# Linear attention in a decoder: the last third of a group's TensorE order is rewritten

## The reference, cut to what matters

```
q, k = split(x @ Wq.T), split(x @ Wk.T)             # 4 heads of 32
v    = split(x @ Wv.T)                              # 4 heads of 64
g    = log_sigmoid(x @ Wgk1.T @ Wgk2.T + bgk2) / 32 # decay of every token and channel
A[t, j] = sum_d q[t,d] * k[j,d] * exp(b[t,d] - b[j,d]),  j <= t,  b = cumsum(g)
o = A @ v
o = o * rsqrt(mean(o*o) + eps) * rms_w
x = layernorm(x + (o * silu(x @ Wg.T)) @ Wout.T)
```

## Time and profile before

| | us |
|---|---|
| median of 3 executions | 1483.53 |
| lowest and highest of them | 1474.55, 1489.40 |
| the profiled execution | 1490.95 |
| its span (first to last instruction) | 1489.10 |

### The profile page before, as it was taken

How to read it: one execution, slowest core, us unless ns; L and a number is a source line. 1 busy time by engine, 2 the same in 40 slices (tenths; PEclk the granted TensorE clock), 3 DMA queues, 4 the chain that set the end, 5 groups by cost and what they waited for, 6 DMA issues and landing times.

```text
span 1489.1 us, 63792 instructions
## 1 busy us (share of the span) xinstructions
PE 1276.1 (86%) x26566; PEld 845.5 (57%) x26566; DVE 1211.1 (81%) x2613; ACT 1048.7 (70%) x2244; POOL 801.3 (54%) x1590
## 2 busy tenths in 40 slices
PE   5899898998867777776666699999999999999896
PEld 2566556666544444443333367676766666666685
DVE  2567777676668988887999789999999999999765
ACT  2567676776657888776777667777777777777555
POOL 3366666676657877776888633344433333333133
PEclk8899999999978999888999999999999999999889
DMA  7000000000000000000000000000000000000012
GB/s 201 20 3 3 3 4 2 4 3 4 10 9 24 18 23 19 17 18 2 1 2 2 1 3 3 3 3 3 3 3 17 18 17 24 18 18 10 2 44 72
DMA packets 28671, 24.28 MB, mean 16 GB/s; under 512 B 3676, under 2 KB 23906, under 8 KB 28386
## 3 DMA queue, kind: packets, MB, share of 16 engines
q1 hardware_dynamic: 28386, 20.21, 4.9%
HBM read 15.94 MB, written 4.19 MB: 14 GB/s over the span
## 4 chain that ended last, share of the span: by engine, by line
PE 43%; POOL 23%; issue 18%; DVE 9%; ACT 6%; SPq 0%; POOLq 0%; DMA 0%; DVEq 0%; ACTq 0%
PE keys_T L591 8%; PE keys_O L572 5%; PE keys_O L578 4%; PE keys_E L486 3%; POOL gla_low L1157 3%; PE keys_S L331 3%; POOL cross_pairs L838 3%; POOL cross_spread L805 2%; DVE ffn_hh L2031 2%; PE keys_E L529 2%; POOL gla_gate L1183 2%; ACT keys_pT L658 2%; POOL gla_yg L1190 2%; PE keys_O L598 2%; POOL gla_sq L1177 2%
## 5 line engine op out<-in xcount | busy, mean ns | idle before, releaser
L340 POOL TENSOR_SCALAR keys_spread<-keys_kT,keys_heads 128x512 f32<-128x512 f32 x128 | 86.9, 696 | 230.1 <-ACT keys_kT L622 230.1
L658 ACT ACTIVATE keys_pT<-keys_T 128x512 f32<-128x512 f32 x256 | 152.3, 595 | 76.3 <-PE keys_T L591 73.0
L350 DVE TENSOR_REDUCE keys_mx<-keys_S 128x16 f32<-128x1024 f32 x128 | 156.1, 1219 | 16.4 <-PE keys_S L331 14.6
L591 PE MATMUL keys_T<-ident_sb,keys_pexp 128*128 128x128 f32 x1024 | 165.0, 284 | 3.2 <-ACT keys_pT L658 2.3
L353 DVE TENSOR_TENSOR keys_pe_in<-keys_S,keys_mx 128x1024 f32<-128x1024 f32 x128 | 156.7, 1224 | 4.4
L591 PEld LDWEIGHTS keys_T<-ident_sb,keys_pexp 128*128 128x128 f32 x1024 | 112.6, 141 | 72.5 <-ACT keys_pT L658 38.3
L674 ACT ACTIVATE keys_pexp<-keys_pe_in 128x1024 f32<-128x1024 f32 x128 | 134.7, 1053 | 0.0
L711 DVE RECIPROCAL keys_rinv<-keys_O 128x128 f32<-128x128 f32 x128 | 120.3, 940 | 0.0
L1656 DVE COPY_PREDICATED gla_at<-gla_node,gla_GP 128x256 f32<-128x256 int32 x128 | 65.6, 513 | 61.0 <-ACT gla_at L1502 57.7
L1157 POOL TENSOR_TENSOR gla_low<-gla_ex,gla_kT 128x128 f32<-128x128 f32 x160 | 72.7, 483 | 71.3 <-ACT gla_ex L1493 71.3
L572 PEld LDWEIGHTS keys_O<-keys_pT,keys_vz 128*32 128x32 f32 x4096 | 63.0, 109 | 64.2 <-ACT keys_pT L658 63.8
(11 more groups left out here) (290 smaller groups left out, 3775.2 us busy)
## 6 DMA issues: line engine op xcount, KB each, us to landing
context<-in_ctx_T SPq DMA_DIRECT2D x32, 256.0 KB, 2.7
xs<-in_x SPq DMA_DIRECT2D x8, 512.0 KB, 7.4
out_x<-xs SPq DMA_DIRECT2D x16, 256.0 KB, 2.3
keys_mask_q<-keys_mask_b SPq DMA_DIRECT2D x64, 1.0 KB
keys_bias_right_f<-in_alibi_right SPq DMA_DIRECT2D x1, 512.0 KB, 3.8
ffn_w<-in_L_ffn_w_gate_T SPq DMA_DIRECT2D x1, 256.0 KB, 4.6
ffn_w<-in_L_ffn_w_up_T SPq DMA_DIRECT2D x1, 256.0 KB, 4.7
ffn_w<-in_L_ffn_w_down_T SPq DMA_DIRECT2D x1, 256.0 KB, 5.4
```

Source lines behind the costliest of these rows:

```text
L340: nc.gpsimd.tensor_scalar(spread[:, :, :, j, :].rearrange("q t s k -> q (t s) k"), flat.rearrange("q (a k) -> q a k", k=SEQ), heads[:, j:j ...
L350: nc.vector.tensor_reduce(m, quads(S), X, ALU.max).then_inc(c["mx"], 1)
L591: last = nc.tensor.transpose(T[:, j * P:(j + 1) * P], pexp[:, t % 2, (4 * half + j) * P:(4 * half + j + 1) * P], sh.ident[:, :])
L658: nc.scalar.activation(pT[:, t % 2, 4 * half:4 * half + 4, :].rearrange("q n k -> q (n k)"), T[:, :], ACT.Copy).then_inc(c["pT"], 1)
```

## The change

TensorE: the long product of tile 2 moves from bank EB to bank OB and behind the transposes of the group before; the long product of tile 3 moves behind the decay sums of tile 0; the output product of the group before moves from between the decay sums of tiles 0 and 1 to between two pieces of the next gram, which is issued in levels (0, 1), (2, 3), (4, 5) instead of (0, 1, 2), (3, 4, 5). ScalarE's copies move to match.

```diff
--- before.py
+++ after.py
@@ -1387,8 +1387,6 @@
                     gram(g, p, 1, (2, 3), closes=True)
                 ahead(2)
                 if n:
-                    c.await_nth(pe, "kT", g + 1, 1, 1)
-                    values_and_gates(g + 1, 1 - p, 2, EB)
                     c.await_nth(pe, "vg", g + 1, 2, G)
                 if l:
                     if not n:
@@ -1398,16 +1396,13 @@
                 if n:
                     if m:
                         await_pair(pe, "o", g, 0, 1, 1)
-                    else:
-                        c.await_nth(pe, "vg", g + 1, 1, G)
-                    values_and_gates(g + 1, 1 - p, 3, OB)
-                    c.await_nth(pe, "vg", g + 1, 3, G)
+                    values_and_gates(g + 1, 1 - p, 2, OB)
+                    c.await_nth(pe, "kT", g + 1, 1, 1)
                     if l:
                         await_pair(pe, "yT", g - 1, 1, 1, 1)
                     decay_sums(g + 1, 1 - p, 0)
-                if l:
-                    output(g - 1, 0)
-                if n:
+                    c.await_nth(pe, "vg", g + 1, 3, G)
+                    values_and_gates(g + 1, 1 - p, 3, OB)
                     c.await_nth(pe, "ex", g + 1, 1, G)
                     decay_sums(g + 1, 1 - p, 1)
                 if m:
@@ -1417,10 +1412,14 @@
                 if n:
                     c.await_nth(pe, "ex", g + 1, 2, G)
                     decay_sums(g + 1, 1 - p, 2)
-                    gram(g + 1, 1 - p, 0, (0, 1, 2), opens=True)
+                    gram(g + 1, 1 - p, 0, (0, 1), opens=True)
+                if l:
+                    output(g - 1, 0)
+                if n:
+                    gram(g + 1, 1 - p, 0, (2, 3))
                     c.await_nth(pe, "ex", g + 1, 3, G)
                     decay_sums(g + 1, 1 - p, 3)
-                    gram(g + 1, 1 - p, 0, (3, 4, 5), closes=True)
+                    gram(g + 1, 1 - p, 0, (4, 5), closes=True)
 
             def drain(n):
                 if n == 0:
```

## The result

The changed kernel takes 1474.9 us (median of 20 executions, 1466.7 to 1486.7) against 1482.2 us (20 executions, 1474.6 to 1489.4). The ratio is 0.9952, 95% interval 0.9934 to 0.997: 7 us less, where no change was forecast. The time lies in the stated range, the direction was not named.

What follows compares the result with a forecast made beforehand. TensorE was taken as the bound in good groups. Eleven good groups at +0.23 us (+2.5) and three late groups (-2.5) summed to 0, so the median 1483.53 was rounded up to 1484 us, range 1473 to 1493.

Steps and rivals of the forecast that it cites:

- The tail of a good group: TensorE, gram's end to next body: mix at 4.70 us, held by `place`; `turn_x` at 11.02, before 10.79; POOL's waits leave.
- 0.23 us longer per good group, times 11: Good groups of the linear attention: the tail grows from 10.79 to 11.02 us, +2.5 us over 11 groups.
- Late groups, -2.5 us: Three groups with VectorE set-up: an earlier second exponential wins 0.9 us twice and some 0.7 once.
- Together 0: Sum over bodies 1 to 14: good groups +2.5 us and late groups -2.5 us cancel, so no change.
- a rival with a chance of 0.15: Nameless waits before level 5 are instruction supply, catching up while TensorE stands before mix: -4 us, 1480 us; chance 0.15.
- rival A: TensorE's new 0.7 us idle before mix in every group costs the clock, so the kernel is slower; chance 0.05.
- Rival B: Before mix: `place` is no floor, the standstill is absent; -8.7 us with the late groups, 1475 us; chance 0.12.
- Rival D: Small matmul pieces on TensorE: each change of shape costs 0.46 us, 13 us in all, 1496 us; chance 0.07.

Runs made afterwards that it cites:

- output_alone: The kernel before with the output product moved between two pieces of the gram, issued in three, and the long products left in place: ratio 0.999.
- stop_added: The kernel before with one wait more, nothing moved: mix also waits for the second exponential, so TensorE stands ahead of mix in each group: ratio 1.004.
- two_pieces: The changed kernel with the gram in two pieces, levels (0, 1, 2) and (3, 4, 5), instead of three: ratio to the kernel before 0.9962.
- roots_behind_before: The kernel before with ScalarE's two root instructions behind the last exponential in the bodies of groups 4, 6 and 8: ratio 0.9956.
- both_fill128: The changed kernel with the output product in halves, roots behind the last exponential in bodies 4, 6, 8, code shifted 128 instructions: ratio to before 0.985, 1460.5 us.
- shift64_before: The kernel before with its code shifted by 64 instructions, using already satisfied waits at the head of TensorE's program: ratio 0.9951.
- fill128_before: The kernel before with its code shifted by 128 instructions, using 32 small matmuls while the weights load: faster, within 0.5 to 0.65%.
- fill192_before: The kernel before with its code shifted by 192 instructions, using 48 small matmuls while the weights load: faster, within 0.5 to 0.65%.
- shift128_before: The kernel before with its code shifted by 128 instructions, using 256 already satisfied waits at the head of TensorE's program: ratio 0.9942.
- shift192_before: The kernel before with its code shifted by 192 instructions, using 384 already satisfied waits at the head of TensorE's program: ratio 1.002.

## Why the prediction was wrong

- *The tail of a good group*: right. mix at 4.68 for 4.70, the next body at 11.03 for 11.02, the floor is `place`, POOL's wait gone. output_alone fits it too.
- *0.23 us longer per good group, times 11*: the size was off. A good group went from 21.87 to about 21.97. The tail is longer by 0.24 as forecast, but the first part of the body is shorter by 0.17 (10.93 for 11.10): a `turn_x` that waits 0.1 for ScalarE starts when ScalarE has already dealt with `cross`, and the product behind it waits that much less. I had ended my count at `turn_x`.
- *Late groups, -2.5 us*: right in size. The three bodies went from 25.83, 23.41 and 25.28 to 24.88, 22.60 and 24.09, so -2.95 us. With +1.1 for eleven good groups the terms of the sum, as they measured, come to about -2 us; the rest of the 7 was not in it.
- *"Together 0"*: this is the step that failed. The sum priced 14 bodies as good or late and put at nothing, without a reason, the change in the 8.5 us of nameless waits and in the time at a granted clock of 0.5, though both stood in the earlier trace rows as losses. In bodies 0 to 15 they measured -4.8 us (code) and 27.2 to 10.9 us at the low clock, which is 5 to 8 us. The first was a rival with a chance of 0.15 and a mechanism (a stop before mix lets the code catch up) that stop_added speaks against. The second appeared only as a danger from new short stops (rival A). The runs show the reverse: the short stops in every group lowered no clock (0.9563 in stop_added against 0.9537), low stretches stood mostly behind stops of over 1 us, and the changed order has fewer and shorter ones of these.
- *Rival B* had the nearest number (1475 for 1474.9) for a wrong reason: the floor it denied is there. That the time fell into the stated range of 1473 to 1493 is luck, as the range was drawn for the scatter of the median and not for these terms.
- *Rival A*: a low stretch in each of 14 groups would be 14 x (24.32 - 21.89) = 34 us by the earlier trace rows; stop_added, with a stop in each, lost 6. The rival rested on these two stretches. Both are busy to 98%, so they show two levels of the clock and, with the earlier trace rows, a long stop ahead of the lower one; of short stops they show nothing.
- *Rival D*: it took two more changes of shape a group at 0.46 us each. The 0.05 us of the sum for such a change was the author's estimate, and no run shows it by itself. In the changed kernel the two pieces of two levels took 0.79 us each up to the next product (286.16 to 286.95, 288.04 to 288.83), where the sum had 0.77.
- Not thought of: that the same order of work at another position in its code blocks differs by 0.5%. Of the measured 7 us about 4 (plus or minus 3) are the new order at equal position; the other 3 are that the kernel before stood 6 us above the mean of its four positions and the changed one 3 us above that of its own.

What stays open: why the new order waits less for code at equal position (3.6 against 6.2 us on average, and 6.2 against 7.3 at the position where it waits most). The standstill alone doesn't do it, by stop_added; shorter runs of small matmuls would fit, but two_pieces (6.3 against 4.5 and 4.6) is a difference no larger than that between positions. And that long stops cause the low stretches is read from traces, where they come together, and not shown by an experiment that takes away one kind of stop and nothing else: roots_behind_before put waits of 2 us in the place of those it removed, and both_fill128 changed three things at once.

## To carry to other kernels

When a profile has nameless waits on the engine with most instructions, compare their ends with the landings on the instruction queue before pricing an order; if they are waits for code, measure a change at two or more positions of the code (a few idle instructions in front are enough), or half a per cent of luck is taken for a gain. Price the long stops of TensorE first, with the clock after them: here 13 us of stops of 0.9 us, added to every group, cost 6 us (stop_added, which also saved 5 us of waits for POOL), and taking away three late stops, 7 us in sum, gained 6.5, though 4 us of waiting came back elsewhere. And count a moved wait up to the point where the engines meet again, not up to the first instruction of the next body.

## What the runs showed of the hardware

- Code reaches TensorE in blocks of 16 KB, and a wait for one ends 1.19 to 1.64 us after it has landed (203 waits in 20 traces; 212 blocks and 3.47 MB in each). They struck mostly inside the runs of small matmuls (L1310, L1314: 8.0 of 8.4 us in bodies 0 to 15 of before).
- The same program with its code shifted by 64, 128 or 192 instructions ran 0.5 to 0.65% faster (shift64_before, fill128_before, fill192_before).
- Waits that were already satisfied are not free on TensorE, even while nothing else is to be done: 64 more instructions of them (128 waits) started the first matmul 7.05 us later (16.53 us in shift128_before, 23.58 in shift192_before), 0.11 us each.
- Bodies 0 to 15 had 13 us at a granted clock of 0.5 with 14 stops of 0.9 us (stop_added), and 23 to 31 us in the kernel before, with three late stops of 0.9 to 3.2 us and about ten for code of up to 2.0 us. In all 20 traces a low stretch stood behind 7 of 136 stops of 0.6 to 1.0 us, 23 of 33 of 1.5 to 3.0 us and all 9 of 3.0 us and more.
